# The last head group's division: turned by TensorE and divided with tokens on partitions, in place of transfers between layouts

## The reference, cut to what matters

```python
scores = jnp.einsum('bhqd,bhkd->bhqk', q, k) / math.sqrt(hd)      # 32 heads of 16
scores = jnp.where(causal, scores, -jnp.inf)
att = jax.nn.softmax(scores, axis=-1)
out = jnp.einsum('bhqk,bhkd->bhqd', att, v)
out = out.transpose(0, 2, 1, 3).reshape(b, l, d)
return out @ Wo.T + bo
```

## Time and profile before

| | |
|---|---|
| time, three runs | 655.54, 658.32 (median), 666.54 us |
| the profiled execution's own time | 660.1 us |
| its span, first to last instruction | 658.4 us |
| TensorE busy | 611.5 us (93%) |
| VectorE, ScalarE, GpSimd busy | 376.8, 292.7, 77.0 us |
| mean granted TensorE clock | 0.956 of full |

### The profile page before, as it was taken

The page is one execution under the profiler, slowest core; times in us unless marked ns, Lnnn a source line. Parts: engine busy times, 40 slices in busy tenths (PEclk is TensorE's granted clock), DMA queues, the critical chain, the costliest instruction groups (busy, mean ns, idle before and its releaser), DMA issues.

```text
span 658.4 us, 9361 instructions
## 1 busy us (share of the span) xinstructions
PE 611.5 (93%) x3688; PEld 403.6 (61%) x3688; DVE 376.8 (57%) x555; ACT 292.7 (44%) x509; POOL 77.0 (12%) x105
## 2 busy tenths in 40 slices
PE   2999999999999997999889897999999999999993
PEld 2788888878888884776567665435444444445442
DVE  5676644357453329656624544477898778861135
ACT  3456333214432223231201115477787677776750
POOL 3000000000000005003301220111211122121210
...
GB/s 226 125 67 128 95 98 128 32 60 37 65 42 55 65 32 68 121 209 220 66 50 103 128 1 92 142 85 52 114 49 88 86 56 18 30 17 29 17 26 136
DMA packets 24312, 53.67 MB, mean 82 GB/s; under 512 B 8884, under 2 KB 9396, under 8 KB 24260
## 3 DMA queue, kind: packets, MB, share of 16 engines
...
q10 hardware_dynamic: 128, 0.13, 0.1%
...
## 4 chain that ended last, share of the span: by engine, by line
PE 83%; DVE 7%; ACT 5%; issue 2%; DMA 1%; ACTq 0%; SPq 0%; POOLq 0%; POOL 0%; DVEq 0%
PE bank L1200 12%; PE slot L934 10%; PE slot L936 10%; PE slot L935 10%; PE bank L1183 10%; PE bank L934 8%; PE bank L936 7%; PE bank L935 7%; PE slot L1099 6%; ACT probs L912 3%; PE slot L1107 2%; DVE maxcol L1506 2%; DMA stage<-in_stream 1%; PE slot L950 1%; PE slot L1183 1%
## 5 line engine op out<-in xcount | busy, mean ns | idle before, releaser
L912 ACT ACTIVATE probs<-bank 128x512 f32<-128x512 f32 (+2 forms) x294 | 144.5, 563 | 52.5 <-PE bank L1183 49.6
L1506 DVE TENSOR_REDUCE maxcol<-slot 128x2 f32<-128x1024 f32 (+2 forms) x112 | 124.8, 1142 | 43.7 <-PE slot L1107 22.2
L934 PE MATMUL slot<-xt_hi,ring_hi 128*128 128x512 f32 (+2 forms) x248 | 99.8, 402 | 9.2 <-DVE qst L1463 2.5
L936 PE MATMUL slot<-xt_hi,ring_lo 128*128 128x512 f32 (+2 forms) x248 | 99.0, 399 | 0.0
L935 PE MATMUL slot<-xt_lo,ring_hi 128*128 128x512 f32 (+2 forms) x248 | 98.9, 399 | 0.0
L1200 PE MATMUL bank<-probs,v_sb 128*32 128x512 f32 (+3 forms) x768 | 87.1, 528 | 0.7 <-POOL probs L721 0.7
L1183 PE MATMUL bank<-qst,kst 50*128 50x512 f32 (+3 forms) x275 | 76.4, 447 | 4.2 <-ACT probs L912 3.4
L1183 PEld LDWEIGHTS bank<-qst,kst 50*128 50x128 f32 x275 | 35.2, 202 | 62.3 <-ACT probs L912 56.4
L1099 PE MATMUL slot<-kst,qst 48*128 48x512 f32 (+3 forms) x288 | 58.3, 397 | 8.4 <-DVE maxcol L1506 7.6
L721 POOL TENSOR_SCALAR_AFFINE_SELECT probs<-probs 128x512 f32<-128x512 f32 x64 | 42.0, 656 | 203.6 <-ACT probs L912 203.6
L1506 DVE TENSOR_REDUCE maxrest<-slot 128x2 f32<-128x768 f32 (+3 forms) x48 | 49.7, 1044 | 24.0 <-PE slot L1107 23.8
...
## 6 DMA issues: line engine op xcount, KB each, us to landing
...
```

The costliest lines, as they stand in the source:

```text
L912: act.activation(probs[:, to:to + heads, 0:n], score_ps(b)[:, 0:heads * n].rearrange("p (h n) -> p h n", n=n), ACT.Exp, scale=HD ** -0.5). ...
L934: pe.matmul(out_ap, a[0], b[0], start=start, stop=False)
L936: return pe.matmul(out_ap, a[1], b[0], start=False, stop=stop)
L1506: dve.tensor_reduce(per_head[:, :, slots[0]:slots[-1] + 1], scores, AX.X, ALU.max).then_inc(S["max_free"], 1)
```

## The change

Groups 0 to 6 are divided as before, except that group 6, which had been divided together with group 7, is now divided alone in its 64 rows (`divided`), at steps 1 and 9 of group 7. Group 7 no longer goes through `gather`, `invert_den` and `spread_den`, nor through the path of its own at the end. For each half:

- TensorE turns `u_sb` in four transposes of 128 by 128 (`turn_numerators`), so that tokens are on partitions and one PSUM bank holds, for each tile of 128 tokens, the numerators and denominators of the four heads side by side.
- VectorE inverts 16 denominators for each token (4 tiles by 4 heads) and multiplies 256 numerators, into `by_token` (`divide_by_token`). The first 64 columns of `by_token` are zeroed once by GpSimd.
- TensorE turns 128 columns of `by_token` for each tile (`turn_back`), those of the tile being the upper 64, so that the result lands in partitions 64 to 127 (`upper`), the rows that group 7 has in `attn_hi` and `attn_lo`.
- ScalarE makes `attn_hi` (`upper_hi`) and VectorE `attn_lo` (`upper_lo`) straight from PSUM, in 64 rows.

The first half's turn is at step 6 of group 7 ("n"), the turn back at step 7 ("b"), `upper_hi` at step 8 and `upper_lo` at step 9. Both are new users in the rotation of the two slots. The second half's come between and behind the projections of tiles 0 to 3. Tiles 4 and 5 now go to banks 2 and 3, tiles 6 and 7 to the slots again.

```diff
@@ -195,7 +195,12 @@
 SPLIT_AT = {(0, 0): "wo0", (0, 1): "wo1"}
 INVERT_AT = (HT + LAG + 2, LAG + 3)
 DIVIDE_AT = {(g, s): (g // 2 - 1, half) for g in range(2, GROUPS, 2) for half, s in ((0, 1), (1, 9))}
-DIVIDE_AT[GROUPS - 1, STEPS - 2] = (KD - 1, 0)
+DIVIDE_AT[GROUPS - 1, 1] = (KD - 1, 0)
+DIVIDE_AT[GROUPS - 1, 9] = (KD - 1, 1)
+TURN_AT = (GROUPS - 1, HT + LAG)
+TURN_BACK_AT = (GROUPS - 1, HT + LAG + 1)
+UPPER_HI_AT = (GROUPS - 1, HT + LAG + 2)
+UPPER_LO_AT = (GROUPS - 1, HT + LAG + 3)
...
@@ -273,6 +278,10 @@
         todo.append(("m", g + 1, 0))
     if hh == GH - 1:
         todo += [("o", t, k) for t, k in OUT_AT.get((g, s), [])]
+        if (g, s) == TURN_AT:
+            todo.append(("n", 0, 0))
+        if (g, s) == TURN_BACK_AT:
+            todo.append(("b", 0, 0))
...
@@ -292,8 +301,7 @@
         users += [("max", UNITS * g + u) for u in range(UNITS)] + [("q", 2 + g), ("m", g), ("k", 2 + g)]
     users += [(kind, k) for g in range(GROUPS) for s in range(STEPS) for hh in range(GH)
               for kind, k, part in extras(g, s, hh) if kind != "o" or part == 0]
-    users = [(user, (2 * (n % 2), 2 * (n % 2) + 1)) for n, user in enumerate(users)]
-    return users + [(("last", n), (2 * n, 2 * n + 1)) for n in range(2)]
+    return [(user, (2 * (n % 2), 2 * (n % 2) + 1)) for n, user in enumerate(users)]
...

         def o_bank(t):

-            return slot_of(("last", t // 2))[:, t % 2, :] if t < 4 else bank[t - 4][:, :]
+            if t in (HT, HT + 1):
+                return bank[t - 2][:, :]
+            n = t % HT if t < HT else t - HT - 2
+            return slot[n // 2][:, n % 2, :]

...
+        def numerator_ps(half):
+
+            return slot_of(("n", 0))[:, 0, :] if half == 0 else bank[0][:, :]
+
+        def upper_ps(half, part):
+
+            return slot_of(("b", 0))[:, 0, :] if half == 0 else bank[part][:, 0:HALF // 2]
+
+        def upper_columns(half, part):
+
+            return slice(0, HALF) if half == 0 else slice(HALF + part * HALF // 2, HALF + (part + 1) * HALF // 2)
+
+        upper = slice(GH * HD, 2 * GH * HD)
+
+        def divided(m):
+
+            return (slice(0, GH * HD), 2 * m + 1) if m == KD - 1 else (slice(0, P), 2 * m + 2)
...
@@ -653,15 +680,14 @@
                         neg_max(g + 1)
                     if s == INVERT_AT[1] + 1 and g > 0:
                         spread_den(g - 1, 1)
-                    if s == HT + LAG:
+                    if s == HT + LAG and g < GROUPS - 1:
                         gather(g, 0)
-                    if s == INVERT_AT[0] + 1:
+                    if s == INVERT_AT[0] + 1 and g < GROUPS - 1:
                         spread_den(g, 0)
...
-            gather(GROUPS - 1, 1)
...
                 at = slice(half * HALF, (half + 1) * HALF)
-                act.activation(attn_hi[:, m, at], u_all[:, at], ACT.Identity, bias=vec_sb[:, VEC_V + m:VEC_V + m + 1]
-                               ).then_inc(S["attn_hi_ready"], 1)
+                rows = divided(m)[0]
+                act.activation(attn_hi[rows, m, at], u_all[rows, at], ACT.Identity,
+                               bias=vec_sb[rows, VEC_V + m:VEC_V + m + 1]).then_inc(S["attn_hi_ready"], 1)
+
+            def upper_hi(half, part):
+                act.wait_ge(S["b_ready"], half + part + 1)
+                act.activation(attn_hi[upper, KD - 1, upper_columns(half, part)], upper_ps(half, part)[upper],
+                               ACT.Identity, bias=vec_sb[upper, VEC_V + KD - 1:VEC_V + KD]).then_inc(S["upper_hi"], 1)

             project_hi("q", 0)
             act.wait_ge(S["logit_ready"], 3)
...
@@ -1207,6 +1235,26 @@
                 return product(ps, tuple(x[:, k, t * P:(t + 1) * P] for x in (attn_hi, attn_lo)),
                                tuple(x[:, k, :] for x in wo_w), start, stop)
...
+            def turn_numerators(half):
+
+                pe.wait_ge(S["u_free"], 2 * (GROUPS - 1) + half + 1)
+                for t in range(HT):
+                    last = pe.transpose(numerator_ps(half)[:, t * P:(t + 1) * P], u_sb[:, half, t * P:(t + 1) * P],
+                                        ident[:])
+                last.then_inc(S["n_ready"], 1)
+
+            def turn_back(half):
+
+                pe.wait_ge(S["n_free"], half + 1)
+                if half == 0:
+                    pe.wait_ge(S["cleared"], 1)
+                for t in range(HT):
+                    part, at = (0, t) if half == 0 else (t // 2, t % 2)
+                    last = pe.transpose(upper_ps(half, part)[:, at * P:(at + 1) * P],
+                                        by_token[:, GH * HD * t:GH * HD * (t + 2)], ident[:])
+                    if t == HT - 1 or half == 1 and t == 1:
+                        last.then_inc(S["b_ready"], 1)
+
             for g in range(GROUPS):
                 for s in range(STEPS):
                     for hh in range(GH):
...
@@ -1230,13 +1284,20 @@
             for k in range(STEPS * GROUPS - LAG, STEPS * GROUPS):
                 weigh_values(k)
             pe.wait_ge(S["attn_lo_ready"], 2 * KD - 1)
+            pe.wait_ge(S["b_free"], 1)
             pe.wait_ge(S["o_free"], NT)
+            pe.wait_ge(S["exp_done"], banks_before(GROUPS, 0))
             for t in range(HT):
                 out_project(o_bank(t), t, KD - 1, True, True).then_inc(S["last_ready"], 1)
-            pe.wait_ge(S["exp_done"], banks_before(GROUPS, 0))
-            pe.wait_ge(S["u_free"], 2 * GROUPS)
+                if t == 1:
+                    turn_numerators(1)
+            turn_back(1)
+            pe.wait_ge(S["attn_lo_ready"], 2 * KD)
             for t in range(HT, NT):
-                pe.wait_ge(S["last_lo"], t - HT + 1)
+                if t % 2 == 0:
+                    pe.wait_ge(S["b_free"], 2 + (t - HT) // 2)
+                if t >= HT + 2:
+                    pe.wait_ge(S["out_sb_ready"], t - HT - 1)
                 out_project(o_bank(t), t, KD - 1, True, True).then_inc(S["last_ready"], 1)

...
-                dve.wait_ge(S[f"u_landed{half}"], 64 * (2 * m + 2))
-                dve.wait_ge(S[f"den_spread{half}"], 16 * (2 * m + 2))
-                dve.tensor_tensor(u_all[:, at], u_all[:, at], den_all[:, at], ALU.mult).then_inc(S["attn_f"], 1)
+                rows, groups = divided(m)
+                dve.wait_ge(S[f"u_landed{half}"], 64 * groups)
+                dve.wait_ge(S[f"den_spread{half}"], 16 * groups)
+                dve.tensor_tensor(u_all[rows, at], u_all[rows, at], den_all[rows, at], ALU.mult
+                                  ).then_inc(S["attn_f"], 1)
+
+            def divide_by_token(half):
+
+                dve.wait_ge(S["n_ready"], half + 1)
+                if half == 1:
+                    dve.wait_ge(S["b_ready"], 1)
+                ps = numerator_ps(half)
+                then(dve.reciprocal(inverse[:].rearrange("p (a b) -> p a b", b=2), wide(ps[:, HD:], (4 * HD, 2 * HT), (HD, 2))))
+                dve.tensor_tensor(by_token[:, GH * HD:].rearrange("p (a b d) -> p a b d", b=2, d=HD),
+                                  wide(ps, (4 * HD, 2 * HT), (3 * HD, 2), (1, HD)),
+                                  wide(inverse[:], (2, 2 * HT), (1, 2), (0, HD)), ALU.mult).then_inc(S["n_free"], 1)
+
+            def upper_lo(half, part):
+
+                at = upper_columns(half, part)
+                dve.wait_ge(S["upper_hi"], half + part + 1)
+                dve.scalar_tensor_tensor(attn_lo[upper, KD - 1, at], upper_ps(half, part)[upper],
+                                         vec_sb[upper, VEC_V + KD - 1:VEC_V + KD],
+                                         attn_hi[upper, KD - 1, at].bitcast(F32), ALU.add, ALU.subtract
+                                         ).then_inc(S["b_free"], 1)
...
@@ -1566,42 +1650,35 @@
...
                                 negate_max(u)
+                            elif kind == "n":
...
+                    if (g, s) == UPPER_LO_AT:
+                        upper_lo(0, 0)
...
-            attn_split_lo(KD - 1, 0)

             def take_out_project(t):
                 dve.wait_ge(S["last_ready"], t + 1)
                 dve.tensor_tensor(x_sb[:, t, :], o_bank(t), x_sb[:, t, :], ALU.add).then_inc(S["out_sb_ready"], 1)

             dve.wait_ge(S["o_free"], NT)
-            for t in range(HT):
+            take_out_project(0)
+            divide_by_token(1)
+            take_out_project(1)
+            for n in range(2):
+                upper_lo(1, n)
+            for t in range(2, NT):
                 take_out_project(t)
-            dve.wait_ge(S["last_den"], 16 * GH)
-            dve.wait_ge(S["u_landed1"], 64 * GROUPS)
-            dve.wait_ge(S["den_spread1"], 16 * (GROUPS - 1))
-            for t in range(HT, NT):
-                at = slice(t * P, (t + 1) * P)
-                rows = slice(GH * HD * ((GROUPS - 1) % 2), GH * HD * ((GROUPS - 1) % 2 + 1))
-                then(dve.reciprocal(den_all[rows, at], den_all[rows, at]))
```

(9 more changed lines are left out.)

45 lines of the change are left out of this document (23 added, 22 removed).

## The result

The changed kernel takes 651.35 us, the median of 20 runs (648.44 to 660.34), against 657.7 us for the kernel before, measured beside it on the same chip. The ratio is 0.9921 with a 95% interval of 0.9895 to 0.9947: 0.8% less, or 5.2 us (3.5 to 6.9). The forecast was 651.7 us, with a chance of 0.93 that the time stays within 2%. The profiled execution took 650.89 us.

A forecast was written before the change was run, and what follows sets the result against it. TensorE was taken to bound most of the span, leaving only the last 19.71 us to win. Terms -7.7 (end), +0.2 (store), +0.7 (transposes), +0.24 (ScalarE) gave -6.6, forecast 651.7 us against the median, range 647.5 to 658.5.

The forecast's parts named there:

- The bound: Whole kernel: TensorE is busy for most of the span; only the last 19.71 us offer much to win.
- The end, -7.7: Behind group 7's last product: the last addition ends 9.5 us after the first projection in place of 17.2.
- The store, +0.2: End of the span: the last store takes 0.2 us more than the 2.5 it had.
- The second rival: End: the stores become the bound and move the end by a further 1.1 us, time 652.8; chance 0.10.
- Two bursts in group 7, +0.7: Group 7 on TensorE: two bursts of four transposes add 2 x 0.35 = 0.7 us.
- The cover of the turn back: Group 7, step 7: VectorE's product is ready 1.4 us before TensorE gets to the turn back.
- ScalarE's rounding, +0.24: Group 7 ahead of step 11: a rounding of 0.74 us in a gap of 0.50 costs 0.24.
- Sum: Whole kernel: end, store, transposes and ScalarE together give -6.6 us.
- the range's upper end: Whole kernel: 658.5 us, with 656.9 as upper bound of unknown costs and runs up to +8.2 from their median.
- Half clock at the end: First rival: the clock falls to 1.2 GHz around the end's turn back, +1.6 us, time 653.3; chance 0.13.
- Clock in group 7: Third rival: the clock falls in group 7 from step 6, net +3 us, time 661.3; chance 0.05.
- A wait in group 7: Fourth rival: TensorE waits up to 2 us twice in group 7 for an uncovered chain, 655.7; chance 0.05.

The follow-up runs named there:

- reordered: Changed kernel with tile 0 projected ahead of the last product, tile 2 added in VectorE's gap, step 10's rounding put behind step 11: 647.92 us, ratio 0.982.
- end alone: Changed kernel with group 7's first half divided the old way, only the second half turned: 651.44 us, ratio 0.9905.
- first half alone: Changed kernel with the old end, only group 7's first half turned: 658.64 us, ratio 1.0047.
- end relieved: The reordered kernel with tile 2 added by GpSimd, tile 3 in VectorE's gap, and tiles 4 and 6 started before attn_lo: 649.92 us, ratio 0.9899.
- the repeat: Changed kernel, unaltered, timed again beside the reordered one: 652.11 us, ratio 0.991.
- idle run: Changed kernel with 12 extra VectorE multiplications ahead of the second half's division, so that TensorE stands idle: 663.31 us.

## Why the prediction was right, step by step

**The bound.** Right. Group 7 is TensorE's own pace and the end was not; the change gained in the end alone.

**The end, -7.7.** Measured -8.35 up to the last addition (17.2 to 8.85), so the term was 0.65 too small. Of its steps, turn (1.50), turn back (3.33 for 3.35), inversion (0.26 for 0.25) and multiplication (0.42 for 0.43) came as worked out, the inversion from the same shape out of SBUF and the multiplication by a straight line between rows of other shapes. `upper_hi` and `upper_lo` took 0.83 and 0.89 for the two parts in place of 1.02 each, so the six additions began at 5.18 and not at 5.40; and they overlap a little, 0.60 from start to start (642.33 to 644.73 for four), so that they took 3.67 in place of 4.1. What made the old end long was weighed rightly only as a whole. The text put the moves and the inversions beside each other; taken alone, the moves were worth 1.3 us, since four additions covered them, and the inversions 4.1, of which 0.7 is the last tile's clock. If the two add up, which no run shows, some 2.5 of the 8 are left. They were not isolated; that they lie in the three rounds of ScalarE and VectorE by turns that are gone is argued and not shown.

**The store, +0.2.** Measured +0.4 (2.9 for 2.5). Additions at 0.60 ask for 262144 bytes in 0.60 us, 437 GB/s, and from 644 to 647 the engines moved 375 to 387 at a share of 1.02 to 1.04: the stores no longer quite keep up, and their time to landing grows from 2.0 us to 2.5 over the last six. The second rival lives in the spread of this term, 2.5 (reordered) to 3.5 (end alone) and once 4.8 with a landing of 4.3. It did not decide the result.

**Two bursts in group 7, +0.7.** Measured 0.89 ahead of step 11's scores (25.73 for 24.84 from the group's first score), which is 2 x 0.44: the term was 0.19 too small. The 0.35 was read in the earlier trace rows from the burst's start to the start of the product behind it, and so it is here too; but the pass after that one follows at 0.32 and not at 0.23 (at 0.31 behind the burst of the earlier trace rows), and the reading stopped one pass too early. In the new end, behind the burst at 638.65:

```profile
639.00 0.48 PE L962 MATMUL slot<-xt_hi,attn_hi 128*128 128x512 f32 x1
...
639.32 0.39 PE L963 MATMUL slot<-xt_lo,attn_hi 128*128 128x512 f32 x1
```

The cover of the turn back held: the product was there at 622.31 and TensorE came for it at 624.24, 1.9 us later (1.4 were expected).

**ScalarE's rounding, +0.24.** This term is not borne out, though a size of +0.14 came out not far from it. Scores of step 11 to the last product took 3.51 before and 3.65 after, +0.14. But in the runs where no rounding stands ahead of step 11 (first half alone, reordered, end relieved) they took 3.78, and where it is in its old place with the old first half, 3.59. The difference sits in ScalarE's start: the step's first exponential comes 0.60 behind its first score before (0.59 in the end alone), 0.76 in the changed kernel, close behind the rounding, and 0.86 where no rounding is there and ScalarE stands idle:

```profile
633.26 0.57 ACT L945 ACTIVATE probs<-slot 128x512 f32<-128x512 f32 x1
```

So taking the rounding away doesn't shorten the wait, and the 0.14 can't be put down to it. Why ScalarE starts later with the first half turned stays open.

**Sum.** -7.96 in the end and +1.03 in group 7, -6.93 for the forecast -6.6; by the ratio -5.2 (-3.5 to -6.9). The two agree only at the edge of the interval; the repeat gave -5.9 (-3.9 to -8.0). The stretches ahead of group 7, which wander by 10 us, are the noise in it. That the sum is only 0.3 off is luck in part, since errors of 0.65 in the end and of some 0.2 each in the store and the bursts have opposite signs; that the median of 651.35 is 0.35 from the forecast is more so, with executions between 648 and 660 us. And the range's upper end doesn't follow from its own numbers: 650.7 - 2.8 makes 647.9, near the 647.5 given, but 656.9 + 8.2 makes 665.1 and not 658.5.

**The rivals.** Half clock at the end: clock 1.00 to the last pass; refuted here, and with 8.9 us of transposes too. It would come with idleness: TensorE stood for 0.96 us, and in the run that made it stand for 7.5 the clock fell. The margin was smaller than the prediction took from the old end, where the clock was still full in 644 to 645, 2 to 3 us after TensorE had stopped: in the idle run it fell in the microsecond that began 1.9 us after the stop. Clock in group 7: 1.00 throughout, with three times the transposes as well. A wait in group 7: none ahead of either burst.
